# Four of nine token tiles of a mixture-of-experts output are summed by TensorE, and the rows come in and go out by two tiles

## What is computed

```python
logits = jnp.einsum('bsd,de->bse', input, Wg)
probs = jax.nn.softmax(logits, axis=-1)
top_vals, top_idx = jax.lax.top_k(probs, 2)
top_vals = top_vals / jnp.sum(top_vals, axis=-1, keepdims=True)
...
h = jax.nn.relu(jnp.einsum('ebsd,edh->ebsh', xm, W1) + b1)
y = jnp.einsum('ebsh,ehd->ebsd', h, W2) + b2
out = jnp.sum(y * scores[..., None], axis=0)
...
h = h + _L0_ffn_ref(_layernorm(h), ...)
```

## Time and profile before

| | us |
|---|---|
| median of three runs | 373.53 |
| the three runs | 370.15, 373.53, 374.12 |
| the profiled execution | 371.03 |
| its span in the trace | 369.0 |
| TensorE busy, of the span | 334.8 |
| VectorE busy | 214.6 |
| POOL busy | 130.3 |
| ScalarE busy | 122.1 |
| mean granted clock of TensorE, 1 is full | 0.967 |

### The profile page before, as it was taken

One profiled execution on the slowest core, in us unless ns is written; L12 is line 12 of the kernel. 1 busy time (PEld: TensorE's weight loads), 2 busy tenths in 40 slices (PEclk: granted clock), 3 DMA queues, 4 the chain that ended last, 5 costly groups with the idle time before them and its releaser, 6 DMA issues.

```text
span 369.0 us, 7232 instructions
## 1 busy us (share of the span) xinstructions
PE 334.8 (91%) x2545; PEld 294.1 (80%) x2546; DVE 214.6 (58%) x407; ACT 122.1 (33%) x271; POOL 130.3 (35%) x137
## 2 busy tenths in 40 slices
PE   4999899999999999999998999988899999999900
PEld 3677899999999999999987878854788888888700
DVE  0037679757758685779792128773464454545216
ACT  1026246244343535251432434240223232322300
POOL 5931105333221511314118560003255454554310
PEclk9999699999999999999999999998999999999975
DMA  7950003304102050000000029811112222121156
GB/s 189 332 184 33 0 2 110 120 2 145 42 2 101 2 215 0 2 2 2 2 1 2 2 59 409 302 46 44 44 59 71 73 71 72 57 75 54 43 190 217
DMA packets 16015, 31.13 MB, mean 84 GB/s; under 512 B 2416, under 2 KB 10160, under 8 KB 15728
## 3 DMA queue, kind: packets, MB, share of 16 engines
q1 hardware_dynamic: 13552, 24.15, 18.7%
q0 software_dynamic: 2432, 6.56, 5.9%
HBM read 24.21 MB, written 6.49 MB: 83 GB/s over the span
## 4 chain that ended last, share of the span: by engine, by line
PE 83%; DVE 7%; DMA 5%; issue 3%; SPq 2%; ACT 0%; POOL 0%; POOLq 0%; DVEq 0%
PE ps L819 11%; PE ps L666 9%; PE ps L439 7%; PE ps L575 7%; PE ps L591 7%; PE ps L441 6%; PE ps L440 6%; PE ps L798 3%; PE ps L800 3%; PE ps L799 3%; PE ps L555 3%; PE ps L809 3%; DMA pt<-patches 2%; PE ps L556 2%; PE ps L557 2%
## 5 line engine op out<-in xcount | busy, mean ns | idle before, releaser
L439 PE MATMUL ps<-xnhi,wlo 128*128 128x272 f32 x192 | 58.4, 304 | 1.6 <-DVE xnlo L1132 1.6
L1157 DVE RECIPROCAL invU<-U 128x272 f32<-128x272 f32 x32 | 57.6, 1827 | 0.0
L440 PE MATMUL ps<-xnlo,whi 128*128 128x272 f32 x192 | 56.1, 292 | 0.0
L441 PE MATMUL ps<-xnhi,whi 128*128 128x272 f32 x192 | 56.0, 292 | 0.0
L1031 ACT ACTIVATE hr<-ps,b 128x128 f32<-128x128 f32 x96 | 27.4, 369 | 67.1 <-PE ps L809 67.1
L1508 POOL TENSOR_TENSOR qA<-qraw,invU 128x544 f32<-128x544 f32 x16 | 22.5, 1404 | 71.0 <-DVE invU L1157 36.0
L819 PE MATMUL ps<-w,hr 128*128 x192 | 45.2, 379 | 0.0
L1164 DVE TENSOR_TENSOR pb<-ps,causal 128x592 uint32<-128x592 uint32 (+3 forms) x32 | 27.3, 854 | 28.7 <-PE ps L575 28.5
L1540 POOL DMA_INDIRECT xg<-xrows,gather_u x24 | 24.9, 1038 | 44.1 <-DVE scatter_u L1358 34.1
L439 PEld LDWEIGHTS ps<-xnhi,wlo 128*128 128x128 f32 x192 | 36.9, 192 | 2.4 <-issue 1.7
L1547 POOL DMA_INDIRECT yrows<-yb,scatter_u x24 | 24.5, 1022 | 40.2 <-DVE yb L1398 40.2
(11 more groups left out here) (166 smaller groups left out, 597.4 us busy)
## 6 DMA issues: line engine op xcount, KB each, us to landing
w<-w SPq DMA_DIRECT2D x8, 512.0 KB, 4.3
w<-w SPq DMA_DIRECT2D x1, 4096.0 KB, 13.6
wraw<-w_attn SPq DMA_DIRECT2D x8, 384.5 KB, 3.5
xrows<-xrow SPq DMA_DIRECT2D x16, 128.0 KB, 7.8
yin<-yrows SPq DMA_DIRECT2D x4, 384.0 KB, 4.2
wv<-w_v SPq DMA_DIRECT2D x4, 256.0 KB, 2.6
oT<-w_ot SPq DMA_DIRECT2D x1, 1024.0 KB, 11.9
wo<-w_o SPq DMA_DIRECT2D x2, 512.0 KB, 12.6
```

The source lines that it names most:

```text
L439: pe.matmul(dst, slo, mhi[n], start=(i == 0), stop=False)
L440: pe.matmul(dst, shi, mlo[n], start=False, stop=False)
L441: last = pe.matmul(dst, shi, mhi[n], start=False, stop=(i == len(pairs) - 1))
L1157: dve.reciprocal(invU[:, g * GT:(g + 1) * GT], U[:, g * GT:(g + 1) * GT]).then_inc(s_a, 1)
```

## The change

Groups are now of two tiles, so there are ten loads and five stores: `COMB` is (0,1), (2,3), (4,5), (6,7) and (8). In each of the first four groups TensorE sums the second tile, `TURNED` = 1, 3, 5, 7, and VectorE the first, and tile 8 alone.

For TensorE the shares are made into diagonal matrices: ScalarE multiplies the identity by each share column, eight products of 128 x 128 into `weight` (two picks of four tiles), placed where `at_place` was. A matmul with `weight` scales every row by its share. TensorE puts `hrow` into a PSUM bank with the identity as matrix, runs twelve matmuls of `keep_warm`, and then adds two products for each tile when the loads of its group have landed. ScalarE copies the sum from PSUM over `yin[:, 1, r]`. SyncE stores a group when VectorE's semaphore and ScalarE's (`s_summed`) have both come. VectorE's own two operations on a tile are now interleaved over the groups.

```diff
-COMB = ((0, 3), (3, 6), (6, 8), (8, 9))
+COMB = ((0, 2), (2, 4), (4, 6), (6, 8), (8, 9))
+TURNED = (1, 3, 5, 7)
...
+        start_d = over[0]
         at_place = sb("at_place", [P, A, P], F32R, at=over)
+        weight = nc.alloc_sbuf_tensor_at("weight", [P, len(TURNED), PICKS, P], F32, offset=start_d)
...
+        def sum_bank(r):
+            return {1: 0, 3: 1, 5: 2, 7: 7}[r]
...
             for n, (r0, r1) in enumerate(COMB):
                 sp.wait_ge(s_comb, n + 1)
+                if n < len(TURNED):
+                    sp.wait_ge(s_summed, n + 1)
                 if r1 < RT:
...
             down(NB - 1, 1)
+            for r in TURNED:
+                pe.matmul(ps[:, sum_bank(r), 0:D], ident[:], hrow[:, r], start=True, stop=False)
+            keep_warm(12, 3)
+            pe.wait_ge(s_weight, 1)
+            for n, r in enumerate(TURNED):
+                pe.wait_ge(s_yin[n], 16 * PICKS)
+                for i in range(PICKS):
+                    last = pe.matmul(ps[:, sum_bank(r), 0:D], weight[:, n, i, :], yin[:, i, r], start=False, stop=(i == PICKS - 1))
+                last.then_inc(s_sum, 1)
...
             relu(NB - 1, 1)
+            act.wait_ge(s_share, 1)
+            for n, r in enumerate(TURNED):
+                for i in range(PICKS):
+                    last = act.activation(weight[:, n, i, :], ident[:], ACT.Copy, scale=share[:, r, i:i + 1])
+            last.then_inc(s_weight, 1)
+            for n, r in enumerate(TURNED):
+                act.wait_ge(s_sum, n + 1)
+                act.activation(yin[:, 1, r], ps[:, sum_bank(r), 0:D], ACT.Copy).then_inc(s_summed, 1)
...
             dve.wait_ge(s_share, 1)
-            for n, (r0, r1) in enumerate(COMB):
+            def add_first(n):
+                r = COMB[n][0]
                 dve.wait_ge(s_yin[n], 16 * PICKS)
-                for r in range(r0, r1):
-                    last = dve.scalar_tensor_tensor(yin[:, 0, r], yin[:, 0, r], share[:, r, 0:1], hrow[:, r],
-                                                    ALU.mult, ALU.add)
-                link(last)
-                for r in range(r0, r1):
-                    last = dve.scalar_tensor_tensor(yin[:, 1, r], yin[:, 1, r], share[:, r, 1:2], yin[:, 0, r],
-                                                    ALU.mult, ALU.add)
-                last.then_inc(s_comb, 1)
+                dve.scalar_tensor_tensor(yin[:, 0, r], yin[:, 0, r], share[:, r, 0:1], hrow[:, r],
+                                         ALU.mult, ALU.add).then_inc(s_part, 1)
+
+            def add_second(n):
+                r = COMB[n][0]
+                dve.wait_ge(s_part, n + 1)
+                dve.scalar_tensor_tensor(yin[:, 1, r], yin[:, 1, r], share[:, r, 1:2], yin[:, 0, r],
+                                         ALU.mult, ALU.add).then_inc(s_comb, 1)
+
+            add_first(0)
+            for n in range(1, len(COMB)):
+                add_first(n)
+                add_second(n - 1)
+            add_second(len(COMB) - 1)
```

More of the change, by code:

```diff
@@ L320, in build @@
         s_yin, s_comb = [sem(f"s_yin{i}") for i in range(len(COMB))], sem("s_comb")
+        s_weight, s_sum, s_summed = sem("s_weight"), sem("s_sum"), sem("s_summed")
+        s_part = sem("s_part")
         s_scat = [sem(f"s_scat{i}") for i in range(NY)]
```

## The result

The changed kernel took 369.84 us in the median (369.28 to 371.91, 11 runs), the kernel before 373.53 (370.15 to 374.22, 11 runs). The ratio is 0.9943, with a 95% interval from 0.9917 to 0.9969. A later series of both, on another chip, gave 371.85 against 372.67, ratio 0.9964 (0.9929 to 0.9999). So the change makes the kernel faster by 0.4 to 0.6%, some 1.3 to 2.1 us; the medians of the first series alone would say 3.7.

A forecast was written before the change was run, and what follows sets the result against it. The tail was bound by loads until 361.43 and VectorE behind them; after the change TensorE's queue decides. The last issue moves 366.70 to about 366.6, -0.1 us, so 373.53 - 0.1 = 373.4 us, range 369.5 to 375.7.

The forecast's parts named there:

- The forecast case: Tail: the end stays where it is, since `keep_warm` is queued ahead of the sums; 373.4 us, chance 0.77.
- The steps on TensorE: From 350.03: `hrow` 1.7 us, twelve `keep_warm` 10.4, four sums of 0.87 ending at 365.6, ScalarE's copy at 366.1.
- The eight products for `weight`: ScalarE after its last relu at 347.8: 2.3 us, free under TensorE's 12 us.
- The sum: End of the tail: last store's issue moves from 366.70 to about 366.6, -0.1 us; bounds -0.2 and +1.1.
- The landings and VectorE's end: Tail: groups land at 357.6, 359.1, 360.6, 362.1, single tile 362.9; VectorE's ten operations end at 364.4 to 364.6.
- My bounds for the last tile: Tail loads: the last tile lands between 362.4 and 363.4.
- my two rates: Tail loads: 327 GB/s over the stretch and 376 GB/s in the highest window, with 0.35 MB per us taken between.
- The issue of two more loads: SyncE issues ten loads instead of eight: taken as 0, upper bound 1.1 us.
- The rival of a harmless `keep_warm`: Tail: `keep_warm` runs faster or hides behind late data, so VectorE's 364.6 sets the last store; -2.1 us, 371.4, chance 0.14.
- The rival of a falling clock: Inside `keep_warm`: sums come late; 3.2 us at half clock costs 1.6, giving 375.0; chance 0.09.
- The rule that transposes don't count as busy: Block loop before the tail: by it transposes could let the clock fall early; the prediction took full clock instead.
- fit of 2.0 us for each DMA: Tail loads: 2.0 us plus bytes over 436 GB/s; two more, paid in series, cost 4 us; the prediction rejected it.

The follow-up runs named there:

- `kw24`: The changed kernel with 24 matmuls of `keep_warm` in place of 12; 381.69 us, ratio 1.0252.
- `kw6_two`: The changed kernel with 6 matmuls of `keep_warm` and the second pick's loads issued by ScalarE's queue; 371.11 us, ratio 0.9950 to the kernel before.
- `kw0`: The changed kernel with no `keep_warm` in the tail, the four matmuls of `hrow` kept; 371.80 us, ratio 0.9992.
- `threes_kw6`: The kernel before's groups kept, TensorE summing tiles 2, 5, 7 behind 6 matmuls of `keep_warm`; 372.44 us, ratio 1.0030.
- `best`: The kernel before's groups, loads by two queues, TensorE summing tiles 1, 2, 4, 5, 7 behind 7 matmuls of `keep_warm`; 372.25 us, ratio 1.0006.
- `dve_pairs`: The changed kernel's groups and order, but VectorE sums both tiles and TensorE and ScalarE add nothing in the tail; 372.10 us, ratio 0.9984.

## Why the prediction was right, point by point

**The forecast case holds.** I had 373.4, within 369.5 to 375.7, and "within 1%" at 0.88; measured were 369.84 and, in the later series, 371.85. The steps on TensorE came out one by one: `hrow` 1.73 us (1.7), twelve of `keep_warm` 10.30 (10.4), sums from 361.8 (362.1) with 0.87 us each, the last ending at 365.29 (365.6), ScalarE's last copy to 365.69 (366.1). The start was 0.24 us earlier than in the profile of before, the rest fits within 0.2. The clock stayed at 1.00. The eight products for `weight` took 2.44 us (2.3) under TensorE's work. That `keep_warm` is what the end hangs on is shown by `kw24`.

**The sum was too small.** I moved the last store by 0.1 us; it is 0.29 from the last scatter on (366.70 - 351.37 = 15.33, against 366.19 - 351.15 = 15.04), plus 0.18 less from that store to the end of the execution, a term that the sum didn't have. And in runs of like clock the change is worth 1.2 to 1.4. What was weak in it is the base: I made the sum against one execution's landings. I read from it that VectorE "waits once more until 361.45, and then never waits again", and didn't ask what the end does when that landing moves. In the two profiles of before it takes it over one for one (landing 1.64 us later, tail 1.64 longer), and in the two of the changed kernel it doesn't.

**The landings and VectorE's end.** I had the fourth group at 362.1 and VectorE's end at 364.4 to 364.6; measured were 363.48 and 365.54. The mis-sized term is the time from issue to landing, which I took from an even 0.35 MB per us. From 355 to 363 it was 287 GB/s, and the end was uneven: of the fourth group 31 of the 32 steps had come by 362.73, 0.6 after my 362.1, and the last came another 0.7 later, at 363.45, with the DMA share at 0.04 from 363.0 on. My bounds for the last tile were also wider than my two rates make them, which is 362.6 to 363.2; it landed at 364.14. The issue of two more loads, which I took as 0 with 1.1 as the upper bound, stays open: ten loads land 0.5 us later than eight in the mean of six and five profiles, within their spread, and two queues brought 0.8 in one (`kw6_two`). None of it reached the end, since TensorE's queue was later.

**The rival of a harmless `keep_warm`** was priced wrong for the same reason. I gave it -2.1 us; with 6 matmuls the tail is 0.56 shorter, since the fourth group's landing, with VectorE's operations and the fourth store behind it, comes next.

**The rival of a falling clock** didn't come true in the changed kernel's tail, in either profile. The rule that transposes don't count as busy, in the part on PE-mode transpose of "TensorE: Matmul & The Clock Gate" in the Trainium skill, has nothing in the tail that bears it out: the granted clock was 1.00 from 345 to 350, with the last blocks' transposes in it, and 1.00 through the sums. The Trainium skill's fit of 2.0 us for each DMA, from the anatomy of one DMA in "DMA: Bandwidth & Descriptors", would by my estimate have charged 4 us for the two more loads, paid one after the other. The profiles have ten loads landed 0.5 us later than eight in the mean, within their spread.

**The point estimate against the median** was 3.6 us off in the first series, and the 369.84 lies only 0.3 above the lower end of the range. About 1.2 us are the change. The rest is likely how often the clock fell near 196 and 254, which has nothing to do with the forecast's mechanism; the range held it because it was drawn around the spread of the runs. That much was luck.

## What to carry to other kernels

Work taken off an engine only pays down to the next thing in line: here VectorE's eight operations, 3.4 us, bought 0.5 us between two profiles and 1.2 to 1.4 between runs of like clock, and twelve unread matmuls stood ahead of the ones that replace them. Filler that keeps a clock up should end when the data land: six too many cost 0.56 us here, and a clock that had fallen cost nothing visible in `kw0` and about 0.5 in `threes_kw6`. Such costs are seen only by looking at more than one execution. When a kernel's end hangs on a landing, ask by how much that landing moves between executions: a change that takes the chain off it gains that too.

## What the runs showed of the hardware

- The second group's loads of the same program landed at 10.1 us in one execution and 11.7 in another. In the late one 31 of the group's 32 semaphore steps had come by 9.5 us; one step was 2.2 us behind the rest. In the first the DMA engines moved 327 GB/s over 8.2 us.
- The last scatter landed 2.42 us after its issue in the first profile of before and 3.20 in `best`.
- TensorE's granted clock falls in the middle of the kernel in some executions only, with the same program: the mean clock of the changed kernel's runs stood at 0.980 to 0.995, and two falls go with about 3.0 us (369.69 and 372.69).
- From the last store's issue to the end of the execution it took 4.33 us before, 4.15 to 4.19 in the kernels with four tiles on TensorE, 4.46 in `best`, and 4.94 and 4.25 in the two with three. The time outside the span was 1.97 on average before, 1.99 in `dve_pairs`, 1.86 with three tiles and 1.73 to 1.76 with four or five. What it is, stays open.
